# Mamba mixer and mixture of experts on one core: ScalarE scales both layer norms, and a few small tiles move to PSUM

## The reference

```
def _layernorm(x, eps=1e-05):
    return (x - mean(x)) / sqrt(var(x) + eps)

x = x + mamba(_layernorm(x))         # state-space mixer, 1024 channels, 16 states each
x = x + moe(_layernorm(x))           # 8 experts of 512x1792, the top 2 of each token

# inside mamba, for every token t in order:
h = h * exp(delta[t] * A) + (delta[t] * xc[t]) * B[t]
y[t] = sum over the 16 states of h * C[t]

# inside moe, for every token:
probs = softmax(x @ gate_w);  take the two largest and their indices
```

## Time and profile before

| | |
|---|---|
| time of the kernel, median of 3 runs | 5010.67 us (5009.6 to 5010.82) |
| time of the profiled execution | 5014.11 us |
| its span in the trace | 5012.4 us |
| VectorE busy over the span | 2489.4 us (50%) |
| TensorE busy over the span | 4547.6 us (91%) |
| ScalarE busy | 1802.5 us (36%) |
| GpSimd busy | 1709.4 us (34%) |

### The profile page before, as it was taken

One profiled execution on the slowest core, in us unless ns is written; L12 is line 12 of the kernel. 1 busy time (PEld: TensorE's weight loads), 2 busy tenths in 40 slices (PEclk: granted clock), 3 DMA queues, 4 the chain that ended last, 5 costly groups with the idle time before them and its releaser, 6 DMA issues.

```text
span 5012.4 us, 72320 instructions
## 1 busy us (share of the span) xinstructions
PE 4547.6 (91%) x25508; PEld 3622.2 (72%) x25508; DVE 2489.4 (50%) x3168; ACT 1802.5 (36%) x3684; POOL 1709.4 (34%) x1214
## 2 busy tenths in 40 slices
PE   6788888888888888887499999999999999999999
PEld 5666666666666666665387887888888888888877
DVE  3999999999999999999300000000000000000000
ACT  6667667666767666675100000000000000000000
POOL 3667676666767666675200000000000000000000
PEclk8999999999999999999799999999999999999999
DMA  3111222221122222111310303103030030120300
GB/s 143 68 65 51 76 89 89 85 78 55 52 88 89 85 80 81 52 55 55 115 31 13 105 13 99 19 13 102 16 100 15 15 100 15 42 73 15 102 13 15
DMA packets 132812, 308.52 MB, mean 62 GB/s; under 512 B 8596, under 2 KB 17428, under 8 KB 124308
## 3 DMA queue, kind: packets, MB, share of 16 engines
q1 hardware_dynamic: 116564, 269.55, 15.5%
q0 software_dynamic: 14768, 34.41, 3.6%
q10 hardware_dynamic: 1296, 2.37, 0.1%
HBM read 920.96 MB, written 45.95 MB: 193 GB/s over the span
## 4 chain that ended last, share of the span: by engine, by line
PE 50%; ACTq 0%; DMA 0%; issue 0%; POOL 0%; DVE 0%; ACT 0%; SPq 0%; POOLq 0%; DVEq 0%
PE pA L1240 17%; PE pB L1240 17%; PE pD L1249 16%; PE pX L1227 1%; DMA rows_d<-pad 0%; ACTq L1208 0%; ACTq L1209 0%; DMA xr<-rows_d 0%; POOL out L1113 0%; ACTq L1207 0%; POOL tnum L1101 0%; DVE ow L1334 0%; ACT xT L1211 0%; POOL pad L1094 0%; SPq L1130 0%
## 5 line engine op out<-in xcount | busy, mean ns | idle before, releaser
L393 POOL TENSOR_TENSOR hs<-hs,bc 128x1024 f32<-128x1024 f32 x512 | 1214.0, 2371 | 424.7 <-DVE hs L833 402.5
L708 PE MATMUL pY<-hs,ident 128*128 128x256 f32 x4096 | 1051.5, 407 | 296.9 <-POOL hs L393 296.1
L833 DVE TENSOR_TENSOR_SCAN hs<-dA,pU 128x1024 f32<-128x1024 f32 x512 | 1169.4, 2284 | 28.5 <-DVE pU L823 2.2
L708 PEld LDWEIGHTS pY<-hs,ident 128*128 128x128 f32 x4096 | 801.1, 201 | 520.0 <-POOL hs L393 398.6
L1240 PE MATMUL pA<-xT,w1s 128*128 128x128 f32 x7504 | 992.0, 275 | 0.7 <-ACT xT L1211 0.7
L1240 PE MATMUL pB<-xT,w3s 128*128 128x128 f32 x7504 | 991.8, 275 | 0.0
L1198 ACT ACTIVATE gate<-pA 128x512 f32<-128x512 f32 (+1 forms) x268 | 145.8, 544 | 2310.1 <-PE pB L1240 2310.1
L1240 PEld LDWEIGHTS pA<-xT,w1s 128*128 128x128 f32 x7504 | 919.2, 192 | 32.7 <-issue 31.6
L1113 POOL DMA_INDIRECT out<-ow,trow x67 | 104.6, 1561 | 2437.2 <-DVE ow L1334 2400.5
L455 ACT ACTIVATE dA<-delta,aneg 128x255 f32<-128x255 f32 x2048 | 849.2, 509 | 221.7 <-DVE hs L833 206.7
L1240 PEld LDWEIGHTS pB<-xT,w3s 128*128 128x128 f32 x7504 | 914.1, 192 | 0.0
(11 more groups left out here) (162 smaller groups left out, 2373.8 us busy)
## 6 DMA issues: line engine op xcount, KB each, us to landing
w1s<-in_w SPq DMA_DIRECT2D x204, 1024.0 KB
w3s<-in_w SPq DMA_DIRECT2D x204, 1024.0 KB
w2s<-in_w SPq DMA_DIRECT2D x204, 1024.0 KB
win<-in_w_in SPq DMA_DIRECT2D x64, 1024.0 KB, 5.2
bc<-bc_d SPq DMA_DIRECT2D x64, 1024.0 KB, 4.7
w1s<-in_w SPq DMA_DIRECT2D x68, 512.0 KB
w3s<-in_w SPq DMA_DIRECT2D x68, 512.0 KB
w2s<-in_w SPq DMA_DIRECT2D x68, 512.0 KB
```

The lines of the kernel that those rows point to most:

```text
L393: pool.tensor_tensor(hs[b][:, :, :], hs[b][:, :, :], bc[:, N + g * PN:N + (g + 1) * PN, :], ALU.mult)\
L708: m = pe.matmul(pY[c % 2][:, 0:T], ident[:, :], hs[k % NB][:, i, :], start=False, stop=g == UPC - 1 and h == PPU - 1 and i == PN - 1)
L833: dve.tensor_tensor_scan(hs[b][:, :, :].rearrange("p n t -> p (n t)"), dA[b][:, :, :].rearrange("p n t -> p (n t)"), pU[:, :, :].rearrange ...
```

## The change

VectorE no longer scales the rows of either layer norm. A helper `scales` (two small instructions) leaves the factor `rs` and the offset `nb` = -mean * factor in SBUF, and ScalarE scales with one activation per tile, Identity with a bias and a scale per partition. For the first norm ScalarE does it at the step's end, behind its part of softplus; for the second in slot 10, behind the copy of `dtr`. The refinement of the second norm begins at (8, 1), behind the first scan of slot 8, instead of (8, 3), and `scales` stands at (9, 3). ScalarE's root reads the variance itself and adds epsilon as its bias. The tile for variance plus epsilon, two tiles of the refinement and a copy `ohp` of the first one-hot lie in PSUM now, and `sel` is added from `ohp`.

```diff
-        ve = [sb(f"ve_{i}", [P, TT]) for i in range(2)]
-        nt_ = [sb(f"nt_{i}", [P, TT]) for i in range(2)]
+        nb = [sb(f"nb_{i}", [P, TT]) for i in range(2)]
+        y_ = [sb(f"y_{i}", [P, TT]) for i in range(2)]
...
-        tiny1 = [ve[0], sd[0], small(TT), nt_[0], rs[0]]
-        tiny2 = [ve[1], sd[1], small(TT), nt_[1], rs[1]]
+        ohp = small(TT * E, E)
+        tiny1 = [small(TT), sd[0], y_[0], small(TT), small(TT)]
+        tiny2 = [small(TT), sd[1], y_[1], small(TT), small(TT)]
...
         def _(act):
+            def normalise1(n):
+                ge(act, scale1, n + 1)
+                for t in range(TT):
+                    act.activation(xf[:, t, :], xf[:, t, :], ACT.Identity, bias=nb[0][:, t:t + 1],
+                                   scale=rs[0][:, t:t + 1]).then_inc(xn1, 1)
...
-                        act.activation(tiny2[1][:, :], tiny2[0][:, :], ACT.Sqrt).then_inc(sd2, 1)
+                        act.activation(tiny2[1][:, :], mv2[:, :, 1], ACT.Sqrt, bias=series[:, 2:3]).then_inc(sd2, 1)
...
                     if u == 10 and back:
+                        ge(act, scale2, r + 1)
+                        ge(act, scattered, 16 * 2 * TT * r)
+                        for t in range(TT):
+                            act.activation(rows[0][:, t, 0:D], xb[:, t, :], ACT.Identity, bias=nb[1][:, t:t + 1],
+                                           scale=rs[1][:, t:t + 1]).then_inc(xn2, 1)
                         ge(act, logits_mm, r)
...
+                if ln1:
+                    normalise1(f + 1)
                 beside(SLOTS - 1)
...
+            act.wait_ge(consts_set, NSET)
             act.wait_ge(var1, 1)
...
             act.wait_ge(a_neg, 1)
+            normalise1(0)
...
-            def normalise(dst, src, mv, tiny, t):
-                return dve.tensor_scalar(dst, src, mv[:, t, 0:1], tiny[4][:, t:t + 1], ALU.subtract, ALU.mult)
+            def scales(ch, mv, tiny, n, ready):
+                ch.settle()
+                ch.done(dve.tensor_copy(rs[n][:, :], tiny[4][:, :]))
+                dve.scalar_tensor_tensor(nb[n][:, :], tiny[4][:, :], -1.0, mv[:, :, 0], ALU.mult, ALU.mult)\
+                   .then_inc(ready, 1)
...
                 if i == 8:
-                    ch.settle()
-                    for t in range(TT):
-                        normalise(xf[:, t, :], xf[:, t, :], mv1, tiny1, t).then_inc(xn1, 1)
+                    scales(ch, mv1, tiny1, 0, scale1)
...
                     if i == 6:
+                        bk.done(dve.tensor_copy(ohp[:, :, :], oh[0][:, :, :]))
...
-                        dve.tensor_tensor(sel[:, :, :], oh[0][:, :, :], oh[1][:, :, :], ALU.add).then_inc(sel_ready, 1)
+                        dve.tensor_tensor(sel[:, :, :], ohp[:, :, :], oh[1][:, :, :], ALU.add).then_inc(sel_ready, 1)
...
-                        if at == (8, 3):
+                        if at == (8, 1):
                             ge(dve, sd2, r + 1)
                             newton(bk, tiny2, 0)
-                        if at in ((9, 0), (9, 1), (9, 3)):
-                            newton(bk, tiny2, 1 + (0, 1, 3).index(g))
-                        if at == (10, 0):
-                            bk.settle()
-                            ge(dve, scattered, 16 * 2 * TT * r)
-                            for t in range(TT):
-                                normalise(rows[0][:, t, 0:D], xb[:, t, :], mv2, tiny2, t).then_inc(xn2, 1)
+                        if at in ((8, 3), (9, 0), (9, 1)):
+                            newton(bk, tiny2, 1 + ((8, 3), (9, 0), (9, 1)).index(at))
+                        if at == (9, 3):
+                            scales(bk, mv2, tiny2, 1, scale2)
```

More of the change, by code:

```diff
@@ L115, in mixer @@
         tabled = sb("tabled", [P, 1])
-        series = sb("series", [P, 2])
+        series = sb("series", [P, 3])
         dtr = sb("dtr", [P, T])
@@ L219, in mixer @@
         xn2 = sem("xn2")
+        scale1 = sem("scale1")
+        scale2 = sem("scale2")
         second_rows = sem("second_rows")
@@ L237, in mixer @@
         NCONST, NWEIGHTS = 4, 5
-        NSET = 11 + NB
-        LN1S, BACKS, SPS, LNS = 7, 34, 4, 5
+        NSET = 12 + NB
+        LN1S, BACKS, SPS, LNS = 8, 36, 4, 5
         CONVS = (5 * PAIRS, 4 * PAIRS)
@@ L353, in _ @@
                 pool.memset(dA[b][:, :, 0:1], 0.0).then_inc(consts_set, 1)
-            for i, v in enumerate((LN1P_SHIFT, LN1P_SMALL)):
+            for i, v in enumerate((LN1P_SHIFT, LN1P_SMALL, EPS)):
                 pool.memset(series[:, i:i + 1], v).then_inc(consts_set, 1)
-            pool.wait_ge(consts_set, 5 + NB)
+            pool.wait_ge(consts_set, 6 + NB)
             pool.affine_select(out=ident[:, :], in_=ident[:, :], compare_op=ALU.not_equal, fill=1.0, base=0,
@@ L520, in beside @@
                         ge(act, var1, s + 3)
-                        act.activation(tiny1[1][:, :], tiny1[0][:, :], ACT.Sqrt).then_inc(sd1, 1)
+                        act.activation(tiny1[1][:, :], mv1[:, :, 1], ACT.Sqrt, bias=series[:, 2:3]).then_inc(sd1, 1)
                     if 13 <= u <= 15 and front:
@@ L567, in step @@
                     act.activation(tabled[:, :], ones[:, 0:1], ACT.Exp)
+            act.wait_ge(consts_set, NSET)
             act.wait_ge(var1, 1)
-            act.activation(tiny1[1][:, :], tiny1[0][:, :], ACT.Sqrt).then_inc(sd1, 1)
+            act.activation(tiny1[1][:, :], mv1[:, :, 1], ACT.Sqrt, bias=series[:, 2:3]).then_inc(sd1, 1)
             act.wait_ge(consts_in, 16 * NCONST)
-            act.wait_ge(consts_set, NSET)
             act.activation(aneg[:, :, :], aneg[:, :, :], ACT.Exp).then_inc(a_exp, 1)
```

## The result

The changed kernel takes 4979.95 us (median of 4 runs, 4976.43 to 4982.87), the kernel before 5010.74 in the same session. The ratio is 0.994, with a 95% interval of 0.9927 to 0.9953. It is faster, by 30.8 us. The forecast was 4968 with a range of 4946 to 4992. The profiled execution took 4976.43 us, 37.7 less than the profiled one of before; the sum of the prediction said 42.3 for this pair.

The account below looks back on a forecast made before the run. VectorE was taken to set the pace. Terms 10.1 + 8.0 + 16.5 + 11.2 - 1.0 - 2.5 gave 42.3 us, 5014.1 to 4971.8 in the profile, a median of 4968, range 4946 to 4992.

Parts of the forecast that it names:

- four signs of being wrong: Logits copy not waiting, variance over 0.3 us, TensorE's granted clock below 1.00 in slots 10 and 11, VectorE awaiting the root.
- Second norm at the gate: Slots 8 to 11: VectorE freed of 2.7 us (even) or 1.75 (odd), mostly lost waiting for TensorE's gate product; 10.1 gained.
- that rival, given 8%: TensorE, waiting before turning rows, falls to 1.2 GHz from dtr to the gate's end: about +100 us, 5068; 8%.
- The chain ahead of the gate: Slots 8 to 11: work before the gate product starts earlier only by the variance part, 1.0 us even, 0.55 odd.
- Gate product: TensorE's product that the logits copy waits for: net later by 0.17 us in even and 0.62 in odd steps.
- Variance of the first norm: Writing to PSUM frees this VectorE instruction from GpSimd: 1.02 and 0.51 us fall to about 0.2, 8.0 us gained.
- Sum of one-hots: VectorE's 128x16 sum falls from 2.23 to 0.16 us in eight odd steps: 16.5 us gained.
- End of the step: VectorE's scalings go, but softplus is then held behind GpSimd's weighing: 0.8 us gained in 14 steps, 11.2.
- Start and tail: Prologue loses 2.2 us to scaled tiles and a turning, the last step 0.3 to extra hand-over: cost 2.5.
- The rival of a new code stall: VectorE's longer loop body brings a second stall like the back edge's, costing 25 us in six passes: 4993; 8%.

Follow-up runs that it names:

- e5: The kernel before with only the change's PSUM parts (variances, reciprocal-chain links, one-hot copy), epsilon in ScalarE's root, both scalings kept on VectorE: 4975.56 us.
- e2: The changed kernel with the second norm's scaling back on VectorE at the start of slot 10: 4973.56 us.
- e3: The changed kernel with the first norm's scaling back on VectorE at the step's end: 4983.42 us.
- e7: e4 with the first softplus product of 128x1024 written to PSUM, its two inputs still in SBUF: 4953.77 us.
- e8: e4 with the last routing part (two casts and the token count) ahead of the first softplus product instead of behind it: 4955.54 us.
- e6: The changed kernel with only the first of ScalarE's two row scalings moved one slot sooner, behind the bcs copy: 4961.34 us.
- e10: e9 with the last routing part ahead of softplus too, as in e8: 4935.79 us.
- e9: e4 with VectorE's first residual sum one place later, behind the scan of the same piece: 4939.64 us.
- e4: The changed kernel with both of ScalarE's row scalings one slot sooner, behind the bcs copy instead of the dtr copy: 4953.51 us.

## Why the prediction was right, point by point

The time, the sign and the main mechanism held, and one of its four signs of being wrong came true: the granted clock in slots 10 and 11 was 0.79 in step 4. Term by term, of the profiled pair:

- **Second norm at the gate: 10.1 said, 6.4 measured** (32.8 - 27.1 in steps 0 to 14, and 0.7 in step 15). VectorE's own gain was 2.8 in even and 1.9 in odd steps (said 2.7 and 1.75). Where the clock holds, the even steps keep 0.92 to 1.03 (said 0.97) and most odd steps 0.91 (said 1.18). What the sum left out is the clock: that rival, given 8%, came true in part. The prediction priced it at about 7.5 us a step, from `dtr` to the gate's end; measured are 1.7 in steps 4, 6, 8 and 12 each (3.44 of wait instead of 1.75), 6.8, and 1.6 more in step 1, because only the skip and state products ran slow and the gate product kept its 1.85. Against that, steps 2, 7 and 13, to which I gave 0.1 at most, kept about 1 us each.
- **The chain ahead of the gate** was said to come 1.0 sooner in every even step. In steps 2, 6 and 12 of the kernel before the `dtr` copy stood 1.4 to 1.7 us later in the step than in step 4 (91.8 to 92.2 us from the step's start against 90.4); in the changed kernel it stands at 89.4 in all four. So in the three steps that had no margin the chain came forward by about 2.5 to 2.8.
- **Gate product: +0.17 in even steps said, +0.12 measured** (in step 10 it stands 7.00 us after the `dtr` copy instead of 5.80, and that copy came 1.08 sooner). This agreement is luck in part. "So I take 0.55 for a tile of 512" was too short, a tile takes 0.75 or 0.80, and the turning moved by 1.39 us against the `dtr` copy (1.19 behind its start, before 0.20 ahead of it) and not by 1.17. The state products gave 0.2 of that back, since they no longer wait and take 3.62 us instead of 3.83.
- **Variance of the first norm, with the copy to PSUM in the same column: 8.0 - 1.0 = 7.0 said, 6.7 measured**, a net 0.79 in even and 0.16 in odd steps.
- **Sum of one-hots: 16.5 said and 16.6 measured**, 2.07 in each of eight odd steps, confirmed by e5. The column's 16.7 for seven steps is something else by 2.2: in steps 1, 3, 5, 7, 9 and 11 the kernel before waits 0.29 us at its L900 for nothing visible, the changed kernel does not, and e2, whose column is -14.6, waits 0.25 at another instruction (L834) in the same steps. Nobody foresaw this term, and no run isolates it.
- **End of the step: 11.2 said, 11.2 measured**, and e3 gives it back. The hold behind the weighing (1.08) was carried from step 14 and holds in every step; e7 and e8 confirm that it ends with GpSimd's instruction.
- **Start and tail: 2.5 lost said, 1.3 lost measured**, 0.64 in the prologue and as much behind the last scan.
- **Not in the sum:** the step's start (+2.0, the back-edge stall 23.3 instead of 21.2) and slots 0 to 7 (+1.7, and 0.4 in step 15). The rival of a new code stall priced 25 for it; no second stall came. With these the terms add up to the 37.7 us of the pair.

Prologue +0.6, the table's other columns -36.6 and the stretch from step 15 on -1.7 make -37.7. The other 7 us between this and the medians (30.8) are the spread of single executions: the profiled one of before was 3.4 above its median and the changed one 3.5 below. So the pair flatters the prediction: by the medians the kernel gained 30.8 us where 42.7 were forecast.

The ScalarE tile deserves a sentence of its own, since a row was at hand and misled me: 1.05 us for 128x1024 in the earlier trace rows is a copy without scale or bias from SBUF tiles. The trace of e6 shows 0.80 us for a tile of 512 with both. The Trainium skill has it ("ScalarE: Activation LUTs", "What ACT_TABLE_LOAD costs"): 186 ns, 0.833 ns an element and 93 ns for each per-partition pointer, an estimate of 0.80 for this tile. The trace agrees.

What is left open: what decides in which steps the clock falls, why the back-edge stall differs between kernels (16.1 to 24.0 us in five passes), where most of e10's lead over e9 comes from, and whether e2 is really faster than the changed kernel.

## What to carry to other kernels

Moving an instruction from the busiest engine to an idle one pays only if the idle engine does it before the chain behind it needs it: here the same scaling, one slot sooner on ScalarE, turned 5.7 kept us into 30.5. First look for instructions on the busiest engine that last longer than their size: freeing three tiny ones (e5) was worth as much as the whole change. And when a wait disappears, look up the next wait on the same engine: the residual sum moved by one place gave another 14 us, and the best version stands at 4935.8, 74 us below the kernel before, where the change had 31.

## What the runs showed of the hardware

- A product of two SBUF inputs is held by GpSimd's instruction even with its result in PSUM (3.18 us for 1.2, e7), while a one-input instruction with a PSUM result is not (0.15 us beside GpSimd's 2.37).
- A softplus product of two SBUF inputs that VectorE began while GpSimd weighed ended 1.08 to 1.10 us behind GpSimd's instruction in each of steps 0 to 14 (changed kernel, e4, e7, e8).
- The same two waits of TensorE (1.22 and 0.84 us) were followed by a granted clock of 0.79 in step 4 and of 1.00 in step 10, with all engines equally busy in the 6 us ahead of it. What the products behind such waits take is not a property of the code alone.
- The prologue is +0.3 us in e4, +0.6 in the changed kernel, +2.7 in e9 and +3.0 in e6, with the same instructions in all four. One profile can't price a change of 2 us there.
